# First attention: rotary queries from the 64-wide latent on two row tiles, and normalized rows ahead of their products

## The chip, the cores and the metric

The kernel runs on one core of a Trainium2 chip. The metric is the device time of one execution in microseconds, as the median of several runs.

## The reference

Four attention layers alternate with four feed-forward layers over 16 sequences of 256 tokens, 128 wide, each followed by a residual and a layer norm. The change is in the first attention:

```python
kv_c = x @ W_kv                                  # 32 wide
kv_c = kv_c * rsqrt(mean(kv_c * kv_c) + EPS) * g_kv
q_c = x @ W_q                                    # 64 wide, the query latent
k_content, v = heads(kv_c @ W_kdec, 8), heads(kv_c @ W_vdec, 8)
q_content = heads(q_c @ W_qdec, 8)
k_rope, q_rope = rope(heads(x @ W_krope, 32)), rope(heads(q_c @ W_qrope, 32))
q, k = concat(q_content, q_rope), concat(k_content, k_rope)
attn = softmax(where(causal, q @ k / sqrt(40), -inf))
x = layernorm(x + (attn @ v) @ W_o)
```

`rope(t) = t * cos + rotate_half(t) * sin`: the kernel multiplies by the weights and by the same weights with their halves swapped, multiplies each result by its table, and adds.

## The kernel before

X holds the tokens as 32 tiles of 128 rows and XT the same turned; the eight PSUM banks are four for scores (`sbank`), two for turned probabilities (`tbank`), one for values (`O`) and one for projections (`PRE`).

`opening_stage` loads the constants, the weights `l0_kv` and `l0_fold` and X in four parts. PE folds products of weights (W_q with the content part and with both rotary matrices, 128 x 640 and 128 x 512, in banks 5 to 7) and DVE copies them out. PE then transposes X in eight groups of four tiles, ACT copies them to XT, and the small latents give the root mean squares `rkv`. The last three groups reuse the banks of the fold and wait for its copies.

`narrow_stage` runs the attention. A sequence has three quads of four units: quads 0 and 1 take the late query tile (two heads of 256 keys per unit), quad 2 the early one (four heads of 128 keys). The loops run over 16 sequences, two in an iteration of the hardware loop, with one slot per quad. Every engine has its own instruction stream, in an order written out by hand in its `slot` function; semaphores join them, and all counts are offset by the constant CREDIT (1).

In a slot, PE issues the scores of its quad (`scores`, L747), the values of the quad two slots back, and the turns of the probabilities of the quad one slot back (`turn`, two before and two at the end of the slot). Between these stand the twelve steps that prepare the next sequence, four in each quad at places 0 to 3. `LatentNarrow` lists them: rms (root mean squares, spread over the rows), cq (content queries), ck (content keys), q and k (rotary queries and keys in four chunks each, two matmuls of 256 columns per step), v (values). Even steps use bank `PRE` (lane 0, `step_out0`), odd ones bank `sbank[0]` (lane 1, `step_out1`), so the scores of a slot wait until the lane-1 step before them has been read. ACT copies rms and cq out, DVE the others: for q and k one multiplication by the table of a whole bank into `tt` (two buffers), which POOL adds into `q` or `kx`.

DVE's slot: masks of units 0 and 1, step place 0, mask 2, place 1, mask 3, place 2, then what a finished tile of rows needs, and place 3. A tile `e` goes through four things in consecutive slots: its values are gathered and its denominators turned (`denominators`, DVE `recip`); POOL repeats the reciprocals, PE turns them (`repeat_turn`), and DVE multiplies the rows by them (`norm`, L923, into the one buffer `on`); PE projects them (`project`, L812), and DVE adds the residual (`residual`). Tiles end in quads 1 and 2. The two waits that matter here are in `norm` and `project`:

```python
dve.wait_ge(S["projected"], 4 * i + e + CREDIT)       # norm(e): tile e-1 is projected
pe.wait_ge(S["normed"], 4 * i + e + 1 + CREDIT)       # project(e)
```

`norm(e)` and `repeat_turn(e)` stand in quads 1 and 2, `project(e)` and `residual(e)` one slot later, in quads 2 and 0. So quad 2 holds the norm of one tile and the projection of the tile before. PE's order there is place 3, `repeat_turn`, `project`, turns 2 and 3; DVE's is place 2, place 3, `norm`, `residual`. The scores of the next slot wait for the residual and the norm that precede them, since banks 2 and 3 are used for them. POOL subtracts the row maxima of four units (`shift`) with the steps' adds between, and at the end of quad 2 copies the inputs of the sequence after next.

Of the kernel before, what the change touches and what calls it, by code (L numbers as in the profile page):

```python
# [139 lines left out]
def place_weights(items, region_cols):  # L140
# [257 lines left out]
def opening_stage(core, ctx, F, rkv, next_weights=()):  # L398
# [9 lines left out]
    with ExitStack() as mem:  # L408
# [10 lines left out]
        for name, rows, cols in (("wqT", 64, 128), ("wqall", 64, 640), ("wqrot", 64, 512), ("wkvT", 32, 128), ("wkdec", 32, 128),  # L419
                                 ("wvdec", 32, 128), ("gkv", 32, 1)):  # L420
            fold[name] = all_fold[0:rows, at:at + cols]
            at += cols
# [70 lines left out]
        def _(dve):  # L493
# [124 lines left out]
def narrow_stage(core, ctx, n, hd, steps, epilogue, next_weights=(), head_bias=False, weights_of=None):  # L618
# [13 lines left out]
    with mem:  # L632
# [111 lines left out]
        def _(pe):  # L744
# [92 lines left out]
            def step(i, b, j, first=False):  # L837

                seq = 2 * i + b
                if not first:  # L840
                    pe.wait_ge(S[steps.out_of(j)], steps.nth_out(seq, j) - 1 + CREDIT)
                    if j % lanes:
                        masks_done(i, b * NQ - NQ + j * NQ // NS, 0)
                elif j >= len(FIRST):
                    pe.wait_ge(S[steps.out_of(j)], steps.nth_out(0, j - len(FIRST)) + CREDIT)
# [11 lines left out]
            def slot(i, s):  # L857
# [19 lines left out]
                for e in ending(i, s, LRT):  # L877
                    repeat_turn(i, s, e)
# [12 lines left out]
        def _(dve):  # L891
# [62 lines left out]
            def step(i, b, j, first=False):  # L954
                seq = 2 * i + b
                if steps.engine[j] == "dve":
# [4 lines left out]
                    if steps.roped and steps.kinds[j] in "qk":  # L961
                        dve.wait_ge(S["rope_added"], seq * steps.ropes + max(steps.rank(j) - 1, 0) + CREDIT)
# [19 lines left out]
            def slot(i, s):  # L982
# [5 lines left out]
                if in_loop(i):  # L988
# [3 lines left out]
                    if lanes == 2:  # L992
                        steps_in(i, s, 2)
# [7 lines left out]
                for e in ending(i, s, LRT):  # L1001
                    norm(i, e)
# [147 lines left out]
class NarrowSteps:  # L1150
# [3 lines left out]
    ropes = 0  # L1154
    content = False
# [26 lines left out]
    def nth_out(self, seq, j):  # L1182
        return seq * (self.count // self.lanes) + j // self.lanes + 1

# [118 lines left out]
class LatentNarrow(NarrowSteps):  # L1303
# [5 lines left out]
    lanes = 2  # L1309

    def __init__(self, hd, rkv, F):
        self.kinds = ["rms", "cq", "ck"] + ["q", "q", "k", "k"] * 2 + ["v"]
        self.engine = ["act", "act", "dve"] + ["dve"] * 9
        self.hd, self.rkv, self.F = hd, rkv, F

    def alloc(self, sb, sem, B, S):
# [5 lines left out]
        B["tt"] = [sb(f"tt{i}", [P, 2, SEQ]) for i in range(2)]  # L1322
        B["rms_diagonal"] = [sb(f"rms_diagonal{i}", [P, 2, P]) for i in range(2)]
        B["rms"] = [sb(f"rms{i}", [P, SEQ]) for i in range(2)]
# [11 lines left out]
    def wait_q_and_k(self, pe, S, seq, q):  # L1336
        if q == 0:
            pe.wait_ge(S["k_ready"], seq + 1 + CREDIT)
            pe.wait_ge(S["rope_added"], 8 * seq + 4 + CREDIT)
# [3 lines left out]

    def pe(self, pe, core, B, S, PRE, j, b, seq):
        kind, F, xs = self.kinds[j], self.F, B["xs"][b]
        if kind == "rms":
            pe.wait_ge(S["diagonal"], seq + 1 + CREDIT)
            return pe.matmul(PRE[:, 0:SEQ], core.const("ones"), B["rms_diagonal"][b][:, :, :], start=True, stop=True)
        if kind in ("cq", "ck"):
            w = F["q"][:, 0:P] if kind == "cq" else F["kc"][:, :]  # L1350
            return pe.matmul(PRE[:, 0:SEQ], w, xs[:, :], start=True, stop=True)
# [5 lines left out]
        w = F["q"][:, P + c:P + c + P] if kind == "q" else weight(core, 0, "l0_wkrope")[:, c:c + P]  # L1357
        rot = F["qrot"][:, c:c + P] if kind == "q" else weight(core, 0, "l0_wkrot")[:, c:c + P]
        pe.matmul(PRE[:, 0:SEQ], w, xs[:, :], start=True, stop=True)
        return pe.matmul(PRE[:, SEQ:2 * SEQ], rot, xs[:, :], start=True, stop=True)  # L1360

    def act(self, act, core, B, S, PRE, j, b, seq):
        if self.kinds[j] == "rms":
            return act.activation(B["rms"][b][:, :], PRE[:, 0:SEQ], ACT.Copy)
        return act.activation(B["qc"][b][:, :], PRE[:, 0:SEQ], ACT.Copy, scale=-1.0 / math.sqrt(40.0))

    def dve(self, dve, core, B, S, PRE, j, b, seq):
        kind = self.kinds[j]
        if kind == "ck":
            dve.wait_ge(S[self.out_of(0)], self.nth_out(seq, 0) + CREDIT)  # L1370
            dve.wait_ge(S["k_ready"], seq + CREDIT)
            return dve.tensor_tensor(B["ck"][:, 0, :], PRE[:, 0:SEQ], B["rms"][b][:, :], ALU.mult)
        if kind == "v":
            for t in range(2):
# [4 lines left out]
        return dve.tensor_tensor(B["tt"][self.rank(j) % 2][:, :, :].rearrange("p a b -> p (a b)"), PRE[:, :],  # L1379
                                 core.const("rope32" + kind), ALU.mult)  # L1380

    def pool(self, pool, core, B, S, j, b, seq):
# [4 lines left out]
        if kind in "qk":  # L1387
            pool.wait_ge(S[self.out_of(j)], self.nth_out(seq, j) + CREDIT)
            tt = B["tt"][self.rank(j) % 2]
            dst = B["q"][b] if kind == "q" else B["kx"][b]  # L1390
# [2236 lines left out]
```

## Time and profile before

| | us |
|---|---|
| median of 3 runs (2693.41 to 2694.88) | 2693.76 |
| the profiled execution | 2698.68 |
| its span, first to last instruction | 2696.9 |
| PE busy | 2321.5 (86%) |
| DVE busy | 1825.7 (68%) |
| ACT busy | 1442.7 (53%) |
| POOL busy | 1354.2 (50%) |

The first attention takes the stretch from the start to about 472 us. The shares are means over all stages; the rows further down are of this stretch. A row of the timeline gives start, duration, engine, line, operation, what is written from what, shapes, the number of instructions merged in it, and in brackets the engine's idle time before it with what ended it. A float32 matmul is two instructions. Matmuls overlap with their successors, so the cost of one is read from the start of what follows and not from its duration; the same holds for DVE, whose operations start before the last one has ended.

### The profile page before, as it was taken

The page shows a single profiled execution, that of the slowest core. Times are in us where ns is not written, and L with a number is a line of the kernel's source. Part 1 is how long each engine was busy: PE and PEld are TensorE (multiplying, and loading weights), DVE is VectorE, ACT ScalarE, POOL GpSimd, SP SyncE. Part 2 cuts the span into 40 slices and gives each one's busy share as a digit, 9 for nine tenths or more (in the row PEclk, how much of TensorE's full clock was granted, in tenths as well). Part 3 has the DMA queues.
Part 4 walks back from the last instruction along what each step waited for, and adds up shares of the span by engine and source line. Part 5 has one row for each costly group of instructions (what it writes and reads, how often), then busy time and mean ns, then how long its engine had stood idle before and what let it go on. Part 6 is the DMA issues. An engine that isn't in the chain of part 4 may idle for free. (4 is left out here: it accounts for less than half of the span.)

```text
span 2696.9 us, 72182 instructions
## 1 busy us (share of the span) xinstructions
PE 2321.5 (86%) x21404; PEld 1819.3 (67%) x21404; DVE 1825.7 (68%) x8013; ACT 1442.7 (53%) x3445; POOL 1354.2 (50%) x1540
## 2 busy tenths in 40 slices
PE   7999999795999925889998889678978999999986
PEld 5777777363676625767776677567766777777755
DVE  4777776563888843568887599846646677777746
ACT  2445444222777713567775466445546666666614
POOL 4778776001777724368885455423314455544501
PEclk8999999796999967899998999899989999999978
DMA  2000000322000014600001000000000000000001
GB/s 76 3 0 0 0 0 0 85 62 100 3 0 0 0 65 137 189 2 1 0 0 41 2 1 0 0 2 1 0 24 1 2 0 0 0 0 0 0 1 32
DMA packets 44039, 55.98 MB, mean 21 GB/s; under 512 B 6800, under 2 KB 29417, under 8 KB 43564
## 3 DMA queue, kind: packets, MB, share of 16 engines
q1 hardware_dynamic: 41580, 49.37, 6.3%
q0 software_dynamic: 2304, 4.79, 0.5%
q8 instruction: 67, 1.10, 0.2%
q14 instruction: 88, 0.72, 0.1%
HBM read 47.11 MB, written 9.74 MB: 21 GB/s over the span
## 5 line engine op out<-in xcount | busy, mean ns | idle before, releaser
L1110 POOL TENSOR_TENSOR a_sm<-a_sm,a_top 128x512 f32<-128x512 f32 x512 | 521.0, 1042 | 170.7 <-DVE a_top L908 170.6
L908 DVE CUSTOM_DVE_ANT_0 a_sm<-bank,cst 128x128 f32<-128x128 f32 (+1 forms) x1024 | 296.8, 353 | 101.8 <-PE bank L770 84.1
L1033 ACT ACTIVATE a_pr<-a_sm 128x512 f32<-128x512 f32 x512 | 310.3, 629 | 78.7 <-PE bank L784 47.9
L1043 ACT ACTIVATE a_pt<-bank 128x512 f32<-128x512 f32 x432 | 240.5, 591 | 143.4 <-PE bank L784 140.6
L2935 POOL TENSOR_TENSOR a_pr<-a_sm,a_rden 128x512 f32<-128x512 f32 x192 | 197.2, 1049 | 228.3 <-DVE a_rden L2721 227.8
L784 PE MATMUL bank<-cst,a_pr 128*128 128x128 f32 x2304 | 308.2, 277 | 0.6 <-ACT a_pt L1043 0.2
L784 PEld LDWEIGHTS bank<-cst,a_pr 128*128 128x128 f32 x2304 | 257.8, 142 | 31.7 <-issue 20.6
L804 PEld LDWEIGHTS bank<-a_pt,a_v 128*32 128x32 f32 x4608 | 119.1, 110 | 110.8 <-issue 89.3
L2695 DVE CUSTOM_DVE_ANT_0 a_sm<-bank,cst 128x256 f32<-128x256 f32 (+1 forms) x512 | 149.9, 353 | 52.4 <-PE bank L2579 45.2
L804 PE MATMUL bank<-a_pt,a_v 128*32 128x128 f32 x4608 | 156.5, 276 | 29.3 <-issue 22.0
L908 DVE CUSTOM_DVE_ANT_0 a_sm<-bank,a_bias 128x256 f32<-128x256 f32 (+1 forms) x512 | 146.2, 354 | 30.7 <-PE bank L770 28.5
L3011 PE MATMUL bank<-a_xs,W 128*128 128x256 f32 x544 | 141.9, 396 | 16.9 <-ACT a_q L3024 10.8
L2935 POOL TENSOR_TENSOR a5h_pr<-a5h_sm,a5h_rden 128x512 f32<-128x512 f32 x64 | 65.7, 1047 | 149.8 <-DVE a5h_rden L2721 149.8
L908 DVE DVE_READ_ACCUMULATOR2_ANT a_top<- 128x1 f32 x1536 | 128.0, 83 | 0.0
L2841 ACT ACTIVATE a_sm<-a_sm,a_top 128x256 f32<-128x256 f32 x256 | 127.1, 505 | 0.0
L1100 POOL COPY a_xs<-XT 128x256 f32 (+1 forms) x54 | 21.7, 403 | 209.1 <-SPq L632 209.1
L916 DVE COPY a_pt<-bank 128x512 f32<-128x512 f32 x144 | 99.6, 692 | 38.3 <-PE bank L784 34.1
L3011 PEld LDWEIGHTS bank<-a_xs,W 128*128 128x128 f32 x544 | 96.8, 194 | 41.1 <-ACT a_q L3024 17.6
L1048 ACT ACTIVATE a_osb<-bank 128x256 f32<-128x256 f32 (+1 forms) x96 | 43.8, 456 | 145.9 <-PE bank L804 145.9
L770 PE MATMUL bank<-a_kx,a_q 32*128 32x512 f32 (+1 forms) x896 | 111.5, 580 | 9.4 <-DVE a_top L908 4.7
L2855 ACT ACTIVATE a_on<-bank 128x512 f32<-128x512 f32 x64 | 38.3, 598 | 147.3 <-PE bank L2611 147.3
L2579 PE MATMUL bank<-a_k,a_q 64*128 64x256 f32 (+1 forms) x1024 | 98.6, 337 | 17.8 <-ACT a_k L3024 9.4
(492 smaller groups left out, 5937.8 us busy)
## 6 DMA issues: line engine op xcount, KB each, us to landing
f_w<-in_l_w SPq DMA_DIRECT2D x40, 256.0 KB, 3.3
f_spread<-gate_rows SPq DMA_DIRECT2D x16, 512.0 KB, 6.8
W<-in_l_w SPq DMA_DIRECT2D x2, 2048.0 KB, 9.7
x_sorted<-in_l_blank SPq DMA_DIRECT2D x4, 660.0 KB, 7.6
f_xin<-x_sorted SPq DMA_DIRECT2D x10, 264.0 KB
X<-in_x SPq DMA_DIRECT2D x4, 512.0 KB, 7.5
a_bias<-bias_rows SPq DMA_DIRECT2D x1, 2048.0 KB, 7.8
X<-y_rows SPq DMA_DIRECT2D x8, 256.0 KB, 4.9
```

What stands on the lines that cost most here:

```text
L770: mm = pe.matmul(sbank[j][:, col:col + m * kw], B["q"][b][r0:r0 + rows, c, qt * P:(qt + 1) * P], B["kx"][b][r0:r0 + rows, x:x + m, 0:kw], ...
L784: mm = pe.transpose(tbank[j % 2][:, c * P:(c + 1) * P], pr[j][:, c * P:(c + 1) * P], ident)
L804: mm = pe.matmul(O[32 * group:32 * group + 32, blk * P:(blk + 1) * P], B["v"][b][:, kb, hd.slot[h], :], pt[j][:, col:col + P], start=(kb = ...
L908: ins = dve.tensor_tensor_reduce(sm[j][:, m * kw:(m + 1) * kw], sbank[j][:, m * kw:(m + 1) * kw], mk, 1.0, 3.0e38, ALU.add, ALU.min, top[: ...
L916: dve.tensor_copy(pt[j][:, :], tbank[j % 2][:, :]).then_inc(S[f"turned_out{j}"], 1)
L1033: act.activation(pr[j][:, :], sm[j][:, :], ACT.Exp, scale=-1.0).then_inc(S["probs"], 1)
L1043: act.activation(pt[j][:, :], tbank[j % 2][:, :], ACT.Copy).then_inc(S[f"turned_out{j}"], 1)
L1110: pool.tensor_tensor(whole, whole, top[:, qt, a:a + m].unsqueeze(2).to_broadcast([P, m, kw]), ALU.subtract).then_inc(S["shifted"], 1)
L2695: ins = dve.tensor_tensor_reduce(sm[s % 2 * 4 + j][:, m * kw:(m + 1) * kw], sbank[j][:, m * kw:(m + 1) * kw], mk, 1.0, 3.0e38, ALU.add, AL ...
L2841: ins = act.activation(part, part, ACT.Exp, bias=top[:, s % 2, j, m:m + 1], scale=-1.0, accum_out=den[:, s % 2, j, m:m + 1])
L2935: pool.tensor_tensor(pr[j][:, :].rearrange("p (h k) -> p h k", k=kw), sm[q % 2 * 4 + j][:, :].rearrange("p (h k) -> p h k", k=kw), rden[:, ...
L3011: mm = pe.matmul(bank[:, c * SEQ:(c + 1) * SEQ], w[:, a:a + P], xs[:, :], start=True, stop=True)
```

## The change

The rotary queries are no longer computed from the tokens with folded 128-row weights, but in two steps from the latent q_c, 64 wide. `l0_wqq` holds W_q twice, so one matmul of 256 columns in the rms step gives the latent in rows 0 to 63 and again in rows 64 to 127; ACT copies rms and latent out together (`rms_latent`, 512 columns). `l0_wqr` holds the rotary weights in its upper 64 rows and those with swapped halves in its lower 64. `pair` does two chunks at once: four matmuls of 64 rows, alternately on the upper and the lower row tile, each tile into a bank of its own (lane 0 and lane 1). DVE's two products then take one bank each, a table half repeated over both chunks, and POOL adds both chunks in one operation of 512 columns. There are three `tt` buffers instead of two.

The order of the steps becomes rms, cq, q, q in quad 0, ck, k, q, q in quad 1 and k, k, k, v in quad 2. PE issues a pair at place 2 and nothing at place 3; DVE has its two products at places 2 and 3. For this attention `repeat_turn` moves ahead of place 2 on PE and `norm` ahead of place 2 on DVE. The fold of the rotary queries is gone from the opening (two matmuls, two copies), `l0_fold` shrinks from 416 to 160 KB, and only the last transposed group waits for the copies of the fold. Two other attentions use `narrow_stage` with one lane; their order stays.

```diff
 WEIGHTS = {
-    0: [("l0_kv", 128, 36), ("l0_fold", 64, 1665), ("l0_wkrope", 128, 512), ("l0_wkrot", 128, 512),
+    0: [("l0_kv", 128, 36), ("l0_fold", 64, 641), ("l0_wqq", 128, 128), ("l0_wqr", 128, 512), ("l0_wkrope", 128, 512), ("l0_wkrot", 128, 512),
...
@@ opening_stage, PE and DVE @@
-            pe.matmul(bank[5][:, :], fold["wqT"], fold["wqall"][:, P:], start=True, stop=True).then_inc(folded, 1)
-            pe.matmul(bank[6][:, :], fold["wqT"], fold["wqrot"], start=True, stop=True).then_inc(folded, 1)
-            pe.matmul(bank[7][:, 0:P], fold["wqT"], fold["wqall"][:, 0:P], start=True, stop=True)
+            pe.matmul(bank[7][:, 0:P], fold["wqT"], fold["wqdec"], start=True, stop=True)
...
-                if g >= 5:
-                    pe.wait_ge(folded_out, g - 4 + CREDIT)
+                if g == GROUPS - 1:
+                    pe.wait_ge(folded_out, 1 + CREDIT)
...
-            dve.tensor_copy(F["q"][:, P:], bank[5][:, :]).then_inc(folded_out, 1)
-            dve.wait_ge(folded, 2 + CREDIT)
-            dve.tensor_copy(F["qrot"][:, :], bank[6][:, :]).then_inc(folded_out, 1)
-            dve.wait_ge(folded, 3 + CREDIT)
-            dve.tensor_copy(F["q"][:, 0:P], bank[7][:, 0:P])
+            dve.tensor_copy(F["qc"][:, :], bank[7][:, 0:P])
...
@@ narrow_stage, PE: step @@
-                steps.pe(pe, core, B, S, FIRST[j % len(FIRST)] if first else LANE[j % lanes], j, b % 2, seq).then_inc(S["step_mm"], 1)
+                banks = [FIRST[k % len(FIRST)] if first else LANE[k % lanes] for k in together]
+                if len(together) == 2:
+                    steps.pair(pe, B, S, banks, j, b % 2, seq).then_inc(S["step_mm"], 2)
+                elif together:
+                    steps.pe(pe, core, B, S, banks[0], j, b % 2, seq).then_inc(S["step_mm"], 1)
...
@@ narrow_stage, PE: slot @@
+                if lanes == 2:
+                    for e in ending(i, s, LRT):
+                        repeat_turn(i, s, e)
                 if in_loop(i):
                     steps_in(i, s, 2)
...
@@ narrow_stage, DVE: step and slot @@
-                        dve.wait_ge(S["rope_added"], seq * steps.ropes + max(steps.rank(j) - 1, 0) + CREDIT)
+                        dve.wait_ge(S["rope_added"], seq * steps.ropes + max(steps.rank(j) - steps.products + 1, 0) + CREDIT)
...
                     mask(i, s, 3)
-                    if lanes == 2:
+                if lanes == 2:
+                    for e in ending(i, s, LRT):
+                        norm(i, e)
+                    if in_loop(i):
                         steps_in(i, s, 2)
...
@@ LatentNarrow @@
-        self.kinds = ["rms", "cq", "ck"] + ["q", "q", "k", "k"] * 2 + ["v"]
-        self.engine = ["act", "act", "dve"] + ["dve"] * 9
+        self.kinds = ["rms", "cq", "q", "q", "ck", "k", "q", "q", "k", "k", "k", "v"]
+        self.engine = ["act", "act"] + ["dve"] * 10
...
+    def pair(self, pe, B, S, banks, j, b, seq):
+        pe.wait_ge(S[self.out_of(0)], self.nth_out(seq, 0) + CREDIT)
+        for k in range(2):
+            c = self.chunk(j + k) * P
+            for upper in range(2):
+                rows = slice(64 * upper, 64 * upper + 64)
+                mm = pe.matmul(banks[upper][:, k * SEQ:(k + 1) * SEQ], self.wqr[rows, c:c + P],
+                               B["rms_latent"][b][rows, 1, :], start=True, stop=True)
+        return mm
...
@@ LatentNarrow.act, dve and pool @@
-            return act.activation(B["rms"][b][:, :], PRE[:, 0:SEQ], ACT.Copy)
+            return act.activation(B["rms_latent"][b][:, :, :].rearrange("p a t -> p (a t)"), PRE[:, :], ACT.Copy)
...
+        half = self.chunk(j) % 2
+        return dve.tensor_tensor(tt[:, :, :], PRE[:, :].rearrange("p (a b) -> p a b", a=2),
+                                 over(core.const("rope32q")[:, half * SEQ:(half + 1) * SEQ], [P, 2, SEQ], 1), ALU.mult)
...
+        if kind == "q" and self.chunk(j) % 2:
+            c = self.chunk(j)
...
+            pool.tensor_tensor(B["q"][b][:, c - 1:c + 1, :], B["tt"][0][:, :, :], B["tt"][1][:, :, :], ALU.add
+                               ).then_inc(S["rope_added"], 2)
```

## Rows read from the trace of the kernel before

**Rows 1.** The page, its first line.
```profile
span 2696.9 us, 72182 instructions
```

**Rows 2.** Busy time by stretch, first attention: PE, PEld, DVE, ACT, POOL, clock, DMA share, GB/s.
```profile
220.00:260.00 40.00, 39.68 (x431) 31.61 (x424) 30.61 (x139) 20.64 (x42) 33.00 (x39) 1.00 0.00 0
```

**Rows 3.** Waits, 60 to 380 us: waiter, releaser, us in total, times, longest.
```profile
PEld bank L763 <- DVE a_tt L1379: 4.5, 11, 0.4
```

**Rows 4.** Timeline of PE: start, duration, line, operation, matmul instructions, idle before.
```profile
120.60 1.14 PE L763 MATMUL bank<-a_kc,a_qc 32*128 32x512 f32 x8
...
124.71 1.04 PE L784 MATMUL bank<-cst,a_pr 128*128 128x128 f32 x8
125.59 0.60 PE L1351 MATMUL bank<-a_xs,folded_kc 128*128 128x256 f32 x2
...
126.24 0.60 PE L1359 MATMUL bank<-a_xs,folded_q 128*128 128x256 f32 x2
...
127.11 0.61 PE L817 MATMUL bank<-W,a_on 128*128 128x128 f32 x4
...
128.51 1.14 PE L763 MATMUL bank<-a_kc,a_qc 32*128 32x512 f32 x8
...
134.36 0.60 PE L1359 MATMUL bank<-a_xs,W 128*128 128x256 f32 x2
...
137.76 1.14 PE L763 MATMUL bank<-a_kc,a_qc 32*128 32x512 f32 x8 [0.20 <-DVE a_on L926]
...
145.17 0.61 PE L817 MATMUL bank<-W,a_on 128*128 128x128 f32 x4
145.62 1.04 PE L784 MATMUL bank<-cst,a_pr 128*128 128x128 f32 x8
146.77 1.14 PE L763 MATMUL bank<-a_kc,a_qc 32*128 32x512 f32 x8
```

**Rows 5.** Timeline of DVE, the same sequence.
```profile
127.40 0.69 DVE L1379 TENSOR_TENSOR a_tt<-bank,W 128x512 f32<-128x512 f32 x1 [0.40 <-PE bank L1360]
...
128.01 0.28 DVE L344 TENSOR_TENSOR X<-bank,X 128x128 f32 x1
...
137.21 0.41 DVE L926 TENSOR_TENSOR a_on<-a_osb,bank 128x256 f32<-128x256 f32 x1
...
144.79 0.69 DVE L1379 TENSOR_TENSOR a_tt<-bank,W 128x512 f32<-128x512 f32 x1
...
145.40 0.60 DVE L1375 TENSOR_SCALAR a_v<-bank,rkv 128x128 f32<-128x128 f32 x2
...
145.92 0.41 DVE L926 TENSOR_TENSOR a_on<-a_osb,bank 128x256 f32<-128x256 f32 x1
146.25 0.28 DVE L344 TENSOR_TENSOR X<-bank,X 128x128 f32 x1
```

**Rows 6.** Timeline of PE in a later stage, eight matmuls of 64 rows.
```profile
1802.53 2.00 PE L2579 MATMUL bank<-a5h_k,a5h_q 64*128 64x256 f32 x16
1804.46 1.97 PE L2611 MATMUL bank<-a5h_pt,a5h_v 128*64 128x128 f32 x32
```

**Rows 7.** Opening: busy time by stretch, landing of X, timeline of PE and DVE.
```profile
8.00:13.00 5.00, 5.00 (x10) 2.60 (x10) 1.68 (x4) 0.00 (x0) 0.00 (x0) 1.00 1.20 290
18.10:22.20 4.10, 2.67 (x28) 2.19 (x24) 0.00 (x0) 2.17 (x4) 0.00 (x0) 1.00 0.47 177
...
DMA to landing us min/median/max: 6.3/7.5/8.7
...
18.11 1.09 PE L470 MATMUL bank<-cst,X 128*128 128x128 f32 x8
...
26.82 0.35 DVE L513 RECIPROCAL rkv<-open_std 128x32 f32<-128x32 f32 x1 [0.30 <-ACT open_std L490]
```

**Rows 8.** Groups of POOL between 30 and 580 us: busy us, mean ns.
```profile
L1110 POOL TENSOR_TENSOR a_sm<-a_sm,a_top 128x512 f32<-128x512 f32 x192 | 196.6, 1042 | 84.7 <-DVE a_top L908 84.7
...
L1391 POOL TENSOR_TENSOR a_k<-a_tt 128x256 f32<-128x256 f32 x68 | 49.9, 734 | 0.5
```

More of the change, by code:

```diff
@@ L418, in opening_stage @@
         all_fold, at, fold = weight(core, 0, "l0_fold"), 0, {}
-        for name, rows, cols in (("wqT", 64, 128), ("wqall", 64, 640), ("wqrot", 64, 512), ("wkvT", 32, 128), ("wkdec", 32, 128),
-                                 ("wvdec", 32, 128), ("gkv", 32, 1)):
+        for name, rows, cols in (("wqT", 64, 128), ("wqdec", 64, 128), ("wkvT", 32, 128), ("wkdec", 32, 128), ("wvdec", 32, 128),
+                                 ("gkv", 32, 1)):
             fold[name] = all_fold[0:rows, at:at + cols]
@@ L839, in step @@
                 seq = 2 * i + b
[L840 to L845, printed above, removed]
+                together = steps.together(j)
+                for k in together:
+                    if not first:
+                        pe.wait_ge(S[steps.out_of(k)], steps.nth_out(seq, k) - 1 + CREDIT)
+                        if k % lanes:
+                            masks_done(i, b * NQ - NQ + k * NQ // NS, 0)
+                    elif k >= len(FIRST):
+                        pe.wait_ge(S[steps.out_of(k)], steps.nth_out(0, k - len(FIRST)) + CREDIT)
                 if j == 0:
                     pe.wait_ge(S["x_copied"], seq + 1 + CREDIT)
-                steps.pe(pe, core, B, S, FIRST[j % len(FIRST)] if first else LANE[j % lanes], j, b % 2, seq).then_inc(S["step_mm"], 1)
+                banks = [FIRST[k % len(FIRST)] if first else LANE[k % lanes] for k in together]
[3 more added lines that the diff above has]
+                    steps.pe(pe, core, B, S, banks[0], j, b % 2, seq).then_inc(S["step_mm"], 1)
             for j in range(NS):
@@ L876, in slot @@
                     steps_in(i, s, 3)
-                for e in ending(i, s, LRT):
-                    repeat_turn(i, s, e)
+                if lanes == 1:
+                    for e in ending(i, s, LRT):
+                        repeat_turn(i, s, e)
                 if lanes == 2:
@@ L991, in slot @@
                     mask(i, s, 3)
-                    if lanes == 2:
+                if lanes == 2:
+                    for e in ending(i, s, LRT):
+                        norm(i, e)
+                    if in_loop(i):
                         steps_in(i, s, 2)
@@ L1000, in slot @@
                     steps_in(i, s, 3)
-                for e in ending(i, s, LRT):
-                    norm(i, e)
+                if lanes == 1:
+                    for e in ending(i, s, LRT):
+                        norm(i, e)
                 if lanes == 2:
@@ L1154 @@
     ropes = 0
+    products = 2
     content = False
@@ L1183, in nth_out, with together @@
         return seq * (self.count // self.lanes) + j // self.lanes + 1
+    def together(self, j):
+        return [j]
     def rank(self, j):
@@ L1321, in alloc @@
         B["ck"] = sb("ck", [P, 1, SEQ])
-        B["tt"] = [sb(f"tt{i}", [P, 2, SEQ]) for i in range(2)]
+        B["tt"] = [sb(f"tt{i}", [P, 2, SEQ]) for i in range(self.products)]
         B["rms_diagonal"] = [sb(f"rms_diagonal{i}", [P, 2, P]) for i in range(2)]
-        B["rms"] = [sb(f"rms{i}", [P, SEQ]) for i in range(2)]
+        B["rms_latent"] = [sb(f"rms_latent{i}", [P, 2, SEQ]) for i in range(2)]
         S["diagonal"] = sem("diagonal")
@@ L1346, in pe @@
         if kind == "rms":
+            pe.matmul(PRE[:, SEQ:2 * SEQ], weight(core, 0, "l0_wqq"), xs[:, :], start=True, stop=True)
             pe.wait_ge(S["diagonal"], seq + 1 + CREDIT)
@@ L1349, in pe @@
         if kind in ("cq", "ck"):
-            w = F["q"][:, 0:P] if kind == "cq" else F["kc"][:, :]
-            return pe.matmul(PRE[:, 0:SEQ], w, xs[:, :], start=True, stop=True)
+            return pe.matmul(PRE[:, 0:SEQ], F["qc" if kind == "cq" else "kc"][:, :], xs[:, :], start=True, stop=True)
         if kind == "v":
@@ L1371, in dve @@
             dve.wait_ge(S["k_ready"], seq + CREDIT)
-            return dve.tensor_tensor(B["ck"][:, 0, :], PRE[:, 0:SEQ], B["rms"][b][:, :], ALU.mult)
+            return dve.tensor_tensor(B["ck"][:, 0, :], PRE[:, 0:SEQ], B["rms_latent"][b][:, 0, :], ALU.mult)
         if kind == "v":
@@ L3520, in lay_out @@
     qr, kr = v["L0_attn_W_qrope"], v["L0_attn_W_krope"]
-    fold = [v["L0_attn_W_q"].T, content(v["L0_attn_W_qdec"]), qr, half_swapped(qr, 16, 32), v["L0_attn_W_kv"].T,
+    fold = [v["L0_attn_W_q"].T, content(v["L0_attn_W_qdec"]), v["L0_attn_W_kv"].T,
             content(v["L0_attn_W_kdec"]), in_value_order(L0_HEADS, v["L0_attn_W_vdec"]), v["L0_attn_g_kv"].reshape(32, 1)]
```

37 lines of the change are left out of this document (22 added, 15 removed).

## The prediction

> **What bounds the kernel now.** I read the page's first lines for the span [rows 1], then the busy time by stretch [rows 2]: between 220 and 260 us TensorE (PE) is busy 39.68 of 40 us at a granted clock of 1.00, VectorE (DVE) 30.61, GpSimd (POOL) 33.00, ScalarE (ACT) 20.64. The first attention is bound by PE, and DVE and POOL have about a fifth of their time free. The waits [rows 3] show the only PE gap that repeats: 11 times between 60 and 380 us, 4.5 us in all, the head of one quad in three waits for DVE's last product; there the normalization is named too, with 0.20 (the row of 137.76 in [rows 4]). Then I laid one sequence out by PE's starts [rows 4]: quad 0 from 120.60 to 128.51 (7.91 us), quad 1 to 137.76 (9.25), quad 2 to 146.77 (9.01), 26.17 in all, 16 times. Against the same starts stand DVE's last operations of each quad [rows 5].
>
> **Latencies read from these rows.** The last rotary matmul's successor starts at 127.11 [rows 4] and DVE's product of it at 127.40 [rows 5]: 0.29 from the end of streaming to DVE. The normalization ends at 137.21 + 0.41 = 137.62 and the scores start at 137.76: 0.14. After a residual the scores start later: 146.25 + 0.28 = 146.53 to 146.77, 0.24, and 128.01 + 0.28 = 128.29 to 128.51, 0.22. A 128x512 product lasts 0.69 but the next DVE operation starts 0.61 after it (127.40 to 128.01); a normalization takes 0.33 (145.92 to 146.25), the two value operations 0.52 (145.40 to 145.92).
>
> **PE's work.** A rotary step of full height is two 256-column matmuls and takes 127.11 - 126.24 = 0.87 us; four of them carry queries, 3.48 per sequence. The change does two steps as a pair of four matmuls, 64 rows high, on alternate halves of the array. The nearest rows are the eight matmuls of that height and width in a later stage [rows 6]: 1804.46 - 1802.53 = 1.93 us for eight, so 0.97 for four where full height takes 1.74. I take 0.87 of streaming, 0.14 to enter and 0.10 to leave; bounds 0.97 and, if the halves don't overlap, 1.98. The new latent matmul is 256 columns, half a step, 0.43. PE has per sequence 2 x (1.74 - 1.1) - 0.43 = 0.85 us less work.
> The Trainium skill (TensorE: Matmul & The Clock Gate, Part 3) gives a pack the time of one matmul and about 4 ns for each further tile; by that a pair would take 0.87 and the total would be some 3 us lower. The 1.93 us of [rows 6] is above it, and TensorEngine Tiling (Key Properties) says that a change of tiling mode drains the engine, which the pair does twice.
>
> **Quad by quad.** I follow what each quad's end waits for. The scores of the next quad wait for the last lane-1 product, since they write its bank, and for the residual where there is one.
> Quad 0 (latent and rms, content queries, the first pair). Turns 0 and 1 end at 125.59 [rows 4]; the new matmul moves this by 0.43 to 126.02, the pair streams until about 127.0. ScalarE's copy of rms grows from 256 to 512 columns, and its copy of the content queries behind it ends at about 125.9; that is hidden by the same two turns, and if that cover goes it costs the 0.2 it grows. Now DVE: first product at 127.29, reciprocal, 0.17, second product at 128.07, residual at 128.68, end 128.96, scores at 129.19. So 8.59 us instead of 7.91: +0.68. PE alone would be ready at 127.1 + 0.22 + 0.44 + 0.88 + 0.14, about 128.8 (0.22 for the denominators, 126.24 - 126.02; 0.44 for a projection, 145.62 - 145.17; 0.88 for two turns, 125.59 - 124.71).
> Quad 1 (content keys, a key step, the second pair). Turns 0 and 1 end 134.36 - 128.51 = 5.85 into the quad; a query step there becomes the content key matmul (-0.43), the turned reciprocals come ahead (+0.22): 5.64. The pair also needs the key step's product out of bank 0, at about 5.7. It streams until 6.6, products at 6.9 and 7.7 with the reciprocal between, scores at 8.55. Before: 9.25, so -0.70. The normalization, ahead of these products now, falls in DVE's wait for the pair and costs nothing. POOL takes the spread of the content keys (1024 columns, some 1.9 us at a shift's rate) between two of its shifts here; its four shifts of 1.04, an add of 0.73, one of 1.04 for both queries [rows 8] and the spread are about 8.1 us of this quad's 8.55, and the neighbours have 5.5 and 7.4: late by 1.2, with over 2 us before the turns of the next quad want it. Nothing on the path.
> Quad 2 (three key steps, values). Here two tiles meet. The normalization of the late tile waits until the projection of the tile before it has read `on` (there is one buffer), and that projection is issued in this same quad, behind PE's last two steps, ending 145.62 - 137.76 = 7.86 into it [rows 4]. Now the normalization is the last but one thing DVE does (145.92), so the wait hides behind two steps. The change puts it before them. DVE is through its masks by 144.79 at the latest, 7.03 into the quad [rows 5], without the queue behind it having anything to wait for. It now stands until 7.86 + 0.29 = 8.15; queued behind are the third key product, the values and the residual, and behind these the next scores. Normalization to 8.48, product to 9.09, values to 9.61, residual ends 9.89, scores at 10.12: +1.11 over 9.01. It needs an earlier tile, so 15 times.
> Sum for the stage: quad 0, 14 x 0.68 and two without residual at 0.35, +10.2; quad 1, 16 x -0.70 = -11.2; quad 2, 15 x 1.11 = +16.7. Total +15.7. An error of 0.1 in the pair moves it by 3.2.
> The Trainium skill (TensorEngine Tiling, PSUM Bottleneck) warns that tiling speeds TensorE up and not the evacuation of PSUM, which can then become the limit. By it alone quads 0 and 1 would lose what I give them; the rows agree, since the products last 0.69 each and PE has 1.2 to 1.6 us to hide them in.
>
> **The opening.** Two of the fold matmuls and their copies go, and 256 KB of 416 leave the queue ahead of X. At the 290 GB/s of [rows 7] that is 0.9 us. X's parts are issued at 3.23, 3.85 and 4.47 and land 6.3 to 8.7 us later; the third, the slowest, at 13.2, moved up at 12.3. Then come four transposes (0.9) and the first latent matmuls (1.0), so the next transposes start at 14.3 where they start at 18.11 now: -3.8. Between 18.10 and 22.20 PE has 2.67 us of work at a granted 1.00; at half that clock it takes 2.6 longer, and the gain is 1.2. I take -3.3, bounds -1.2 and -4.2.
> **The first sequence's steps**, ahead of the first scores. The latent copy delays the first product, and three products are in flight; POOL's eight adds of 0.73 become four and two of 1.04. Chained by hand from these durations the scores start 0.25 later; bounds -0.4 and +0.8. The two loads added (64 and 256 KB, against 256 taken from another) end long before the stage starts: nothing. The tail: nothing, bound 0.3 either way.
>
> **Total.** +15.7 - 3.3 + 0.25 = +12.6. The profiled execution took 2698.68 us, its span 2696.9 and 1.8 around it; it would become 2711.3. It lies 4.9 above the median of the three runs, 2693.76, so the median becomes 2706.4.
>
> **Rivals.**
> 1. PE's work alone decides, what a count of PE's instructions promises: DVE's products and the normalization stay hidden. Then quad 0 ends at about 8.2 (+0.3), quad 1 at 7.95 (-1.30), quad 2 at 8.87 (-0.14): -1.14 x 16 = -18, with the opening -21, 2672.5. For it speaks PE's 39.68 of 40; against it that DVE reaches the normalization 0.8 us before the projection has ended. It decides for this side if the projection ends more than 1 us earlier in quad 2. Chance 0.06.
> 2. The normalization costs nothing but the pair's products stay exposed: +10.2 - 11.2 - 2 - 3 = -6, 2688. Chance 0.10.
> 3. The half-height matmuls don't overlap: each pair takes 0.9 to 1.0 more, in front of DVE's two products, in quads 0 and 1: +30, 2736. Against it stands the 1.93 us of [rows 6]. Chance 0.05.
> 4. The stall of quad 2 is half of mine (another operation already fills it) and the opening gives its full 4.2: +3, 2697. Chance 0.09.
> The forecast itself has 0.70. Its own range by the bounds of the terms is 2699 to 2714; with rival 4 and the upper pair cost it is 2695 to 2715. What can be told from no change here is 0.2%, 5.4 us. Faster (below 2688.4) has 0.11, same 0.13, slower (above 2699.1) 0.76.
>
> **What would show it.** In the profile after: the scores' wait at the head of quad 0 named after DVE's residual or values, about 1.1 us in 15 of 16; DVE idle before the normalization, released by the projection, about 1.3 us each; quad 1 about 0.7 us shorter; pairs of about 1.0 us; the first transposes before 9 us and the end of the opening by 24. If quad 2 isn't longer, the central step is wrong; if the pairs take 1.9, rival 3.

## The result

The changed kernel takes 2706.35 us (median of 6, 2701.04 to 2707.03) where the kernel before takes 2693.91 (median of 6, 2692.87 to 2697.4): ratio 1.0038, interval 1.0028 to 1.0048. It is slower by 12.4 us. The profiled execution took 2707.03 with a span of 2705.3, 8.35 more than that of before; the profiled execution of before lies 4.8 above its own median, that of after 0.7.

The page's first lines say it as [rows 1] did: PE has less to do (2309.1 us, 2321.5 before), and the span is longer.

```profile
span 2705.3 us, 72259 instructions
## 1 busy us (share of the span) xinstructions
PE 2309.1 (85%) x21434; PEld 1798.9 (66%) x21434; DVE 1818.1 (67%) x8011; ACT 1446.3 (53%) x3445; POOL 1352.0 (50%) x1506
```

The busy time by stretch, PE, PEld, DVE, ACT, POOL, then the clock (the stretch of [rows 2]): PE has gone from 39.68 to 37.20 busy us of 40 at the same clock of 1.00. So PE no longer bounds the first attention throughout.

```profile
220.00:260.00 40.00, 37.20 (x431) 28.70 (x430) 29.43 (x147) 17.79 (x36) 30.30 (x36) 1.00 0.00 0
```

The waits between 60 and 380 us (who waited, for whom, us in total, times, longest) name what stands in its place. [rows 3] had 4.5 us at the head of a quad. Now the scores (L757) wait for three things of DVE, and DVE's normalization (L930) for the projection (L811).

```profile
DVE a_tt L1416 <- PE bank L1391: 25.9, 24, 1.7
...
DVE a_on L930 <- PE bank L811: 13.0, 11, 1.3
...
PEld bank L757 <- DVE a_tt L1416: 10.5, 22, 0.6
...
PE bank L757 <- DVE X L344: 7.3, 6, 1.2
PEld bank L757 <- DVE a_v L1408: 6.4, 5, 1.3
...
PE bank L757 <- DVE a_v L1408: 5.8, 6, 1.1
```

PE's timeline of one sequence, to lay beside [rows 4]. Quad 0 runs from 119.58 to 128.07, quad 1 to 136.53, quad 2 to 146.63: 8.49, 8.46 and 10.10 us, where 7.91, 9.25 and 9.01 stood.

```profile
119.58 1.14 PE L757 MATMUL bank<-a_kc,a_qc 32*128 32x512 f32 x8 [1.08 <-DVE a_v L1408]
...
125.09 1.14 PE L1391 MATMUL bank<-a_rms_latent,W 64*128 64x256 f32 x8
126.16 0.44 PE L820 MATMUL bank<-cst,a_osb 128*128 128x128 f32 x2
...
128.07 1.14 PE L757 MATMUL bank<-a_kc,a_qc 32*128 32x512 f32 x8 [0.16 <-issue]
...
133.80 1.14 PE L1391 MATMUL bank<-a_rms_latent,W 64*128 64x256 f32 x8
134.87 0.44 PE L820 MATMUL bank<-cst,a_osb 128*128 128x128 f32 x2
...
136.53 1.14 PE L757 MATMUL bank<-a_kc,a_qc 32*128 32x512 f32 x8 [0.35 <-DVE a_tt L1416]
...
143.93 0.61 PE L811 MATMUL bank<-W,a_on 128*128 128x128 f32 x4
144.38 1.04 PE L778 MATMUL bank<-cst,a_pr 128*128 128x128 f32 x8
146.63 1.14 PE L757 MATMUL bank<-a_kc,a_qc 32*128 32x512 f32 x8 [1.22 <-DVE X L344]
```

And DVE's, beside [rows 5]. The pair's two products (L1416) and the residual of quad 0; the two products of quad 1; in quad 2 the normalization, the third key product, the values and the residual.

```profile
126.38 0.69 DVE L1416 TENSOR_TENSOR a_tt<-bank,W 128x512 f32<-128x512 f32 x1 [1.71 <-PE bank L1391]
...
127.15 0.63 DVE L1416 TENSOR_TENSOR a_tt<-bank,W 128x512 f32<-128x512 f32 x1
...
127.69 0.28 DVE L344 TENSOR_TENSOR X<-bank,X 128x128 f32 x1
...
135.07 0.69 DVE L1416 TENSOR_TENSOR a_tt<-bank,W 128x512 f32<-128x512 f32 x1 [0.55 <-PE bank L1391]
...
135.84 0.63 DVE L1416 TENSOR_TENSOR a_tt<-bank,W 128x512 f32<-128x512 f32 x1
...
144.65 0.42 DVE L930 TENSOR_TENSOR a_on<-a_osb,bank 128x256 f32<-128x256 f32 x1 [1.17 <-PE bank L811]
144.99 0.68 DVE L1414 TENSOR_TENSOR a_tt<-bank,W 128x512 f32<-128x512 f32 x1
...
145.59 0.60 DVE L1408 TENSOR_SCALAR a_v<-bank,rkv 128x128 f32<-128x128 f32 x2
...
146.11 0.28 DVE L344 TENSOR_TENSOR X<-bank,X 128x128 f32 x1
```

The normalization starts at 144.65, 0.27 after the projection has streamed (144.38), and has waited 1.17 us for it. Third key product, values and residual follow without a gap, the residual ends at 146.39 (146.11 + 0.28), and the scores start 0.24 later; PE had been idle for 1.22 us by then. In quads 0 and 1 the same is seen on a smaller scale: the products start 0.22 and 0.20 after the pair (126.16, 134.87), and the next scores come when the last of them, or the residual behind it, has ended.

The opening and the first scores (L757), against [rows 7]: the transposes (L468) start at 9.04, groups 5 and 6 at 14.64 for 18.11, the opening ends with the reciprocal at 22.08 for 26.82, and the first scores start at 40.02. They started at 43.77 before.

```profile
7.17 0.79 PE L443 MATMUL bank<-W 64*128 64x128 f32 x2 [7.17 <-DMA W<-in_l_fold]
...
9.04 4.53 PE L468 MATMUL bank<-cst,X 128*128 128x128 f32 x20
...
14.64 1.09 PE L468 MATMUL bank<-cst,X 128*128 128x128 f32 x8
...
22.08 0.35 DVE L507 RECIPROCAL rkv<-open_std 128x32 f32<-128x32 f32 x1 [0.29 <-ACT open_std L488]
...
40.02 1.14 PE L757 MATMUL bank<-a_kc,a_qc 32*128 32x512 f32 x8 [3.11 <-POOL a_k L1427]
```

### The profile page after: what moved, and what is told of

Read it like the earlier page. It is cut to its first block and busy times, and to the rows that moved or that the text cites. A ratio compares the mean times of both kernels' runs of the same rounds, so it can differ in the third digit from the quotient of the medians.

```text
span 2705.3 us, 72259 instructions
## 1 busy us (share of the span) xinstructions
PE 2309.1 (85%) x21434; PEld 1798.9 (66%) x21434; DVE 1818.1 (67%) x8011; ACT 1446.3 (53%) x3445; POOL 1352.0 (50%) x1506
## 5 line engine op out<-in xcount | busy, mean ns | idle before, releaser
L778 PE MATMUL bank<-cst,a_pr 128*128 128x128 f32 x2304 | 309.0, 277 | 0.6 <-ACT a_pt L1051 0.4
L778 PEld LDWEIGHTS bank<-cst,a_pr 128*128 128x128 f32 x2304 | 258.3, 142 | 31.7 <-issue 20.6
```

The lines of the kernel that those rows point to most:

```text
L778: mm = pe.transpose(tbank[j % 2][:, c * P:(c + 1) * P], pr[j][:, c * P:(c + 1) * P], ident)
```

## The experiments

Each kernel is compared with the kernel before on the same chip (medians 2694.56 for the first four, 2695.77 for the others). Behind each ratio stands its 95% interval. Differences from the changed kernel are between medians of separate sessions, between which the median of the kernel before itself moved by 0.7 (first four) and 1.9 us (the others). "Quad 0, 1, 2" are the steady distances between the starts of content scores, read off PE's timeline; the sums are over all 16 sequences.

### Two buffers for the normalized rows

```diff
-        on = sb("on", [P, cols])
+        ons = [sb(f"on{k}", [P, cols]) for k in range(lanes)]
...
-                dve.wait_ge(S["projected"], 4 * i + e + CREDIT)
-                dve.tensor_tensor(on[:, :], ...
+                dve.wait_ge(S["projected"], total(i, 4, e + 1 - lanes) + CREDIT)
+                dve.tensor_tensor(ons[e % lanes][:, :], ...
```

> The changed kernel with two buffers for the normalized rows in this attention (even and odd tiles), so that norm(e) waits for the projection of tile e-2 and no longer for e-1, which is issued in the same quad. Theory of the stall (the wait for the projection costs 1.1 us in quad 2, 15 times): quad 2 goes from 10.1 us back to about 9.0, the total from 2706.4 to about 2690 (0.9985 of before), and DVE's idle time before norm named after the projection falls from about 16 us to nearly 0. Rival (the norm costs by its place in DVE's queue alone, 0.33 us ahead of two steps): quad 2 stays above 9.7 and the total at 2701 or more.

Measured: 2688.32 us, ratio 0.9976 (0.9967 to 0.9986), 18.0 less than the changed kernel. Quad 2 went from 10.10 and 9.96, in turn, to 8.89 and 8.81; quads 0 and 1 kept 8.49 and 8.46. DVE's wait for the projection is gone from the list of waits. The timeline, the head of quad 2, its normalization, its projection and the next scores:

```profile
134.30 1.14 PE L757 MATMUL bank<-a_kc,a_qc 32*128 32x512 f32 x8 [0.35 <-DVE a_tt L1416]
...
141.18 0.42 DVE L930 TENSOR_TENSOR a_on<-a_osb,bank 128x256 f32<-128x256 f32 x1
...
141.71 0.61 PE L811 MATMUL bank<-W,a_on 128*128 128x128 f32 x4
...
143.20 1.14 PE L757 MATMUL bank<-a_kc,a_qc 32*128 32x512 f32 x8
```

The normalization (141.18) now starts ahead of the projection (141.71) and not behind it. The one wait that the change had uncovered is worth 18 us in the medians, more than the whole loss of 12.4. The traces say the same: the last residual of the stage is added at 463.40 us and no longer at 480.88. 1.4 of these 17.5 us are already there at the first scores, ahead of every normalization, so what the wait costs by the traces is about 16.

### Norm and turn back at their old places

```diff
 # PE slot
-                if lanes == 2:
-                    for e in ending(i, s, LRT):
-                        repeat_turn(i, s, e)
                 if in_loop(i):
                     steps_in(i, s, 2)
...
                 if in_loop(i) and lanes == 2:
                     steps_in(i, s, 3)
-                if lanes == 1:
-                    for e in ending(i, s, LRT):
-                        repeat_turn(i, s, e)
+                for e in ending(i, s, LRT):
+                    repeat_turn(i, s, e)
...
 # DVE slot
-                if lanes == 2:
-                    for e in ending(i, s, LRT):
-                        norm(i, e)
-                    if in_loop(i):
-                        steps_in(i, s, 2)
+                if in_loop(i) and lanes == 2:
+                    steps_in(i, s, 2)
...
                 if in_loop(i) and lanes == 2:
                     steps_in(i, s, 3)
-                if lanes == 1:
-                    for e in ending(i, s, LRT):
-                        norm(i, e)
+                for e in ending(i, s, LRT):
+                    norm(i, e)
```

> The changed kernel with norm and repeat_turn at their old places (behind place 3), all else as changed. Theory of the stall: quad 2 returns to about 9.0 us (-16.5 in all), quad 1 grows by the 0.33 us of the norm, which now stands between the pair's last product and the next scores (+5): 2695. Rival (the exposed products of the pair are what costs, the move nothing): 2706 as before.

Measured: 2692.93 us, ratio 0.9995 (0.9986 to 1.0005): no difference from before, and 13.4 below the changed kernel. Quad 2 returned to 9.01 to 9.07 and 8.87; quad 1 grew by 0.21 to 8.66, less than the 0.33 expected. So the new steps without the move, opening included, give a gain too small to be told here (1.6 us in the medians; 4.3 at the end of the stage in the traces): what they save in quad 1, 9.4 us in all, they give back in quad 0, 8.9.

### The move alone

```diff
 # PE slot, of the kernel before
+                if lanes == 2:
+                    for e in ending(i, s, LRT):
+                        repeat_turn(i, s, e)
                 if in_loop(i):
                     steps_in(i, s, 2)
...
-                for e in ending(i, s, LRT):
-                    repeat_turn(i, s, e)
+                if lanes == 1:
+                    for e in ending(i, s, LRT):
+                        repeat_turn(i, s, e)
...
 # DVE slot
-                    if lanes == 2:
+                if lanes == 2:
+                    for e in ending(i, s, LRT):
+                        norm(i, e)
+                    if in_loop(i):
                         steps_in(i, s, 2)
...
-                for e in ending(i, s, LRT):
-                    norm(i, e)
+                if lanes == 1:
+                    for e in ending(i, s, LRT):
+                        norm(i, e)
```

> The kernel before with norm and repeat_turn moved ahead of place 2 and nothing else. Theory of the stall: quad 2 grows from 9.0 to 10.1 us (+16.6 in all), quad 1 shrinks by 0.1 to 0.2 (-2): 2708. Rival (in the old order of steps DVE has enough to do, and the move only frees quad 1): 2690 to 2692.

Measured: 2706.24 us, ratio 1.0040 (1.0026 to 1.0054), 11.7 more than the kernel before. Quad 2 is 10.1 and 9.96 as in the changed kernel, quad 1 went from 9.25 to 9.05, quad 0 kept 7.91. The waits of this kernel between 60 and 380 us:

```profile
DVE a_on L930 <- PE bank L817: 13.0, 11, 1.3
...
PE bank L763 <- DVE X L344: 6.2, 5, 1.3
...
PE bank L763 <- DVE a_v L1383: 5.4, 5, 1.1
```

DVE's 13.0 us in 11 times and the scores' waits for residual and values are those of the changed kernel. The stall comes with the move and needs nothing of the new steps.

### Lane 1 first

On top of two buffers, DVE's slot takes the step of the other lane for queries:

```diff
                 for j in steps_at(s, place):
-                    step(i, s // NQ + 1, j)
+                    step(i, s // NQ + 1, j ^ 1 if lanes == 2 and steps.kinds[j] == "q" else j)
```

> The kernel with two buffers for normalized rows, and DVE takes the pair's product out of lane 1 first (the bank that the next scores write), lane 0 second. Theory (the scores wait for the second product alone): quad 1 goes from 8.46 to the time of PE's work, about 7.95 us, 16 times -0.5 = -8; quad 0 keeps its 8.5, since the residual still stands behind both products; 2682. Rival (PE's time per quad is not what would bound quad 1 then; POOL or the turned probabilities are next): quad 1 stays at 8.3 or more, 2688.

Measured: 2683.81 us, ratio 0.9958 (0.9941 to 0.9974), 4.5 less than with two buffers alone. Quad 1 went from 8.46 to 8.10 or 8.13, between the two expectations; quad 0 kept 8.49. Between 60 and 380 us the scores (L757) now wait for no operation of DVE, so quad 1 is as long as PE's work in it, which is 8.10 and not the 7.95 of the expectation.

### The residual between the products

On top of the kernel with two buffers and lane 1 first:

```diff
+                early = lanes == 2 and in_loop(i) and s % NQ == 0
+                if early:
+                    for e in ending(i, s, LY):
+                        residual(i, e)
                 if in_loop(i) and lanes == 2:
                     steps_in(i, s, 3)
...
-                if lanes == 2:
+                if lanes == 2 and not early:
                     for e in ending(i, s, LY):
                         residual(i, e)
```

> As the kernel with two buffers for normalized rows and lane 1 first, and in quad 0 DVE adds the residual between the pair's two products instead of behind both. Theory (quad 0's end is set by the residual): quad 0 goes from 8.49 us to the end of PE's turns, about 8.3, -3 in all, total 2681. Rival (nothing left there): no change, 2684. Against the kernel before about 0.995.

Measured: 2677.76 us, ratio 0.9932 (0.9916 to 0.9949), the fastest of all kernels here, 18.0 us faster than the kernel before on the same chip and 28.6 than the changed kernel. Quad 0 is 8.26. The timeline of the last turns (L778) and the residual of quad 0, then the starts of quads 1, 2 and 0:

```profile
146.27 1.04 PE L778 MATMUL bank<-cst,a_pr 128*128 128x128 f32 x8
...
146.60 0.29 DVE L344 TENSOR_TENSOR X<-bank,X 128x128 f32 x1
...
147.24 1.14 PE L757 MATMUL bank<-a_kc,a_qc 32*128 32x512 f32 x8
...
154.31 1.04 PE L778 MATMUL bank<-cst,a_pr 128*128 128x128 f32 x8
...
155.34 1.14 PE L757 MATMUL bank<-a_kc,a_qc 32*128 32x512 f32 x8
...
164.16 1.14 PE L757 MATMUL bank<-a_kc,a_qc 32*128 32x512 f32 x8
```

The residual (146.60 + 0.29) is done before the last turns have streamed (146.27 + 0.87), and the scores follow these by 0.10. In quad 1 they follow the last turns in the same way (154.31, 155.34). PE bounds all three quads again: between 220 and 260 us it is busy 39.95 of 40. Of the 6.0 us against the kernel of the last section (3 expected) the quads 0 hold 3.5. Most of the rest is one stretch: in that kernel's trace PE is idle for 2.59 us at about 90 us, for nothing that the profile shows, and the clock is 0.76 from 88 to 92; the kernel with two buffers alone has 2.40 us of it at about 91, this one has none. What causes it is open.

### Two product buffers

```diff
-    products = 3
+    products = 2
```

> The changed kernel with two buffers of rotary products instead of three. Theory (the third buffer is needed, because POOL's add of the key step in quad 1 comes behind the spread of the content keys): the pair's second product in quad 1 waits for that add, which ends at about 136.75 in the trace where the product starts at 135.84; quad 1 goes from 8.45 to about 9.4 us, +14 in all, 2720. Rival (POOL is ahead anyway, the third buffer is idle): 2706, no change.

Measured: 2726.62 us, ratio 1.0114 (1.0097 to 1.0131), 20 more than the changed kernel. Quad 1 is 9.45, 1.0 longer, and its 16 add up to 16.6 more; the first quad 0 and the first quad 2 are 1.0 and 1.6 longer, and the first scores start 19.5 us after the opening's reciprocal instead of 17.9. Part of these three is the clock, granted 0.70 between 58 and 62 us where the changed kernel has 1.00. The wait between 60 and 380 us is the expected one, of the pair's product for POOL's add of keys:

```profile
DVE a_tt L1416 <- POOL a_k L1427: 9.4, 11, 0.9
```

### All four matmuls on one half

```diff
-                mm = pe.matmul(banks[upper][:, k * SEQ:(k + 1) * SEQ], self.wqr[rows, c:c + P],
-                               B["rms_latent"][b][rows, 1, :], start=True, stop=True)
+                mm = pe.matmul(banks[upper][:, k * SEQ:(k + 1) * SEQ], self.wqr[0:64, c:c + P],
+                               B["rms_latent"][b][0:64, 1, :], start=True, stop=True)
```

> The changed kernel with all four matmuls of a pair on the lower 64 rows (the rotated half of the queries is computed from the unrotated weights, so that part of the computation is changed). Theory (the two row tiles run at the same time): a pair goes from 1.07 us to about 1.9, in front of DVE's products, so quads 0 and 1 grow by 0.8 to 0.9 each, +27 in all, 2733. Rival (the pair is bound by loading its weights or by changing the tiling, not by streaming): under +8.

Measured: 2738.14 us, ratio 1.0156 (1.0135 to 1.0176). A pair and its successor:

```profile
164.92 1.99 PE L1391 MATMUL bank<-a_rms_latent,W 64*128 64x256 f32 x8
166.84 0.44 PE L820 MATMUL bank<-cst,a_osb 128*128 128x128 f32 x2
```

166.84 - 164.92 = 1.92 us where the changed kernel has 126.16 - 125.09 = 1.07. Quads 0 and 1 are 9.34 and 9.30, 0.84 longer each. The two row tiles do overlap, and the 0.85 us that this saves lies fully on the path. The kernel is 31.8 us slower than the changed one; 26.9 of these are in quads 0 and 1.

### The fold matmuls and the old size of l0_fold

```diff
-    0: [("l0_kv", 128, 36), ("l0_fold", 64, 641), ("l0_wqq", 128, 128), ...
+    0: [("l0_kv", 128, 36), ("l0_fold", 64, 1665), ("l0_wqq", 128, 128), ...
...
+            for k in range(2):
+                pe.matmul(bank[5 + k][:, :], fold["wqT"], all_fold[0:64, 641 + 512 * k:641 + 512 * (k + 1)], start=True, stop=True)
...
```

> The changed kernel with l0_fold at its old 416 KB (the added columns are zeros) and two fold matmuls of 512 columns ahead of the others, into banks that are overwritten later. Theory (the opening's gain is PE's: 3.5 us of matmuls at the lower clock, and 0.7 from the earlier landing of the weights): the first transpose returns from 9.04 to about 13.1 us and the end of the opening from 22.1 to about 26.5; total +4.3. Rival of the prediction (X's landing is what the earlier transposes would meet): the opening ends within 3.8 of the changed kernel's.

Measured: 2709.36 us, ratio 1.0052 (1.0039 to 1.0065). The timeline of its opening:

```profile
8.03 3.78 PE L444 MATMUL bank<-W 64*128 64x512 f32 x4 [8.03 <-DMA W<-in_l_fold]
...
13.31 4.29 PE L470 MATMUL bank<-cst,X 128*128 128x128 f32 x20
...
26.10 0.35 DVE L509 RECIPROCAL rkv<-open_std 128x32 f32<-128x32 f32 x1 [0.29 <-ACT open_std L490]
```

The first transpose is back at 13.31 and the opening ends at 26.10, 4.0 later than in the changed kernel; 3.58 of these are the matmuls (8.03 to 11.61) and 0.86 the later landing of the weights (7.17 to 8.03). By the edge of 3.8 set for the rival this alone is a narrow verdict; clearer is that the changed kernel's transposes start at 9.04, right behind the fold, and not when X's landing would have let them. The median difference, 3.0, is smaller than the 4.0 of the traces, with executions of this kernel between 2703.6 and 2712.1.

## Why the prediction was right, point by point

The sum was 2706.4 and the median 2706.35, but the agreement to a tenth is luck. The stage was sized 2.5 us too high and opening and first steps together 0.7, both in the same direction: in the traces the three add up to +9.5 and not to +12.6. The medians are 12.4 apart because the profiled execution of before lies 4.8 above its own median. The forecast had put the profiled execution of the changed kernel at 2711.3, as far above its median; it took 2707.03, 0.7 above.

**What bounds the kernel.** Before the change PE did, as [rows 2] said. The step that carried the prediction was not PE's count but the order of waits at each quad's end.

**Quad 2.** Predicted +1.11 over 9.01; measured 10.10 and 9.96, in sum +15.5 (predicted 16.7). The prediction took the quad of 9.01 us; the quads alternate between 9.01 and 8.86 before, and both become 1.1 longer. The size for one is right; the count is not. The first quad 2 has no earlier tile and grows by 0.1 (8.61 to 8.67), the next fourteen carry the +15.4, and the last has no further quad behind it: from its scores to the layer norm it is +0.2. Inside the quad the links are as written: the projection ends 7.85 us into it (predicted 7.86), the normalization starts at 8.12 (8.15), the residual ends at 9.86 (9.89). Norm behind the projection, the queue behind the norm and the scores behind that are each seen in the timeline; one kernel takes the stall away with a buffer (-18.0 us), one gives it to the kernel before (+11.7). DVE's wait is 1.17 to 1.18 us each (13.0 in 11), where about 1.3 was named as a sign.

**Quad 0.** Predicted 8.59, measured 8.49. The sum came out as predicted, +10.2, by luck: a steady quad loses 0.58 and not 0.68, 7.5 in thirteen of them, and the first two, for which 0.35 each was taken, lose 2.07 and 0.68. Of the 2.07 some 1.4 are the clock. In this trace PE is idle for 3.11 us ahead of the first scores, the clock is 0.50 between 42 and 44 us, and the first quad 0 takes 8.39. With norm and turn at their old places the first quad, which has neither, holds the same work, PE is idle for 2.94 ahead of it, the clock is 1.00, and the quad takes 6.97 (6.32 before the change). The chain of the steady quad is as written: first product 6.80 us into the quad (6.69 predicted), second 7.57 (7.47), residual 8.11 (8.08). Its last link is shorter: the scores start 0.10 after the residual has ended (127.69 + 0.28 = 127.97, then 128.07), where 0.22 to 0.24 was read from [rows 5]. In quad 2 that link is 0.24 again.

**Quad 1.** Predicted 8.55 and -11.2, measured 8.45 and -12.6. Products at 7.00 and 7.77 (6.9 and 7.7), and the scores 0.06 after the last of them where 0.14 was taken.

**The pair.** 1.07 us (125.09 to 126.16) and 0.10 ahead of it, 1.17, where 1.11 was predicted for both; [rows 6] gave 0.97 for four matmuls inside a run of eight. The row on a later stage was good enough; one half alone takes 1.92, 1.8 times as long. The Trainium skill (TensorEngine Tiling, Overview) gives up to twice as the speedup for a contraction of 64; the trace stays below it. One sum of the prediction is off: by the span model that it names, 0.87 for the pair and not 1.11, the total would be 7.7 lower by its own 3.2 for each 0.1, and not "some 3 us"; nothing else in the forecast used it.

**The stage in sum.** The layer norm behind the stage starts at 474.95 in the trace of before and at 484.43 in that of after; from the first scores to it are 431.2 and 444.4 us: +13.2, predicted +15.7. This term was sized too high by 2.5, 1.2 in quad 2 and 1.4 in quad 1. Without the 1.4 us that the low clock adds to the first quad 0, which was not forecast, it would be +11.8.

**The opening.** Predicted -3.3, measured -4.7 between the two traces and -4.0 against the 26.10 of the kernel with the fold matmuls put back. The step that failed is its mechanism: the landing of X's third part at 12.3 was to set the start of what follows. The twenty transposes start behind the fold at 9.04 and take 4.5 us, 3.7 before; in this trace PE has no idle time for X between them; what the opening gains is PE's 3.6 us and the earlier weights. Groups 5 and 6 start 3.5 us earlier (14.64 for 18.11; predicted 3.8). The other 1.3 us come from the remainder, which took 7.4 us, 8.7 before: it did not slow down after the change, as the branch at the lower clock (-1.2) had it, but was slow before. The clock of before is 0.58 between 22 and 26 us, and its last latents and sums of squares take longer there than the 1.06 and 1.05 of the changed kernel, which has 1.00 up to 22 us:

```profile
22.18 1.55 PE L455 MATMUL bank<-XT,W 128*32 128x512 f32 x8 [0.69 <-ACT XT L484]
...
24.42 1.87 PE L461 MATMUL bank<-W,open_squares 128*128 128x4 f32 x8 [0.70 <-ACT open_squares L488]
```

**The first sequence's steps.** Predicted +0.25 with a bound of +0.8; measured +1.0 (22.08 to 40.02 against 26.82 to 43.77). POOL's add of both queries was sized at 1.04, a shift's time; it takes 1.27. The group of POOL operations:

```profile
L1432 POOL TENSOR_TENSOR a_q<-a_tt 128x512 f32<-128x512 f32 x34 | 43.3, 1273 | 9.2 <-DVE a_tt L1416 9.2
```

Two of these are 0.46 longer than assumed, against the missing 0.75; that both lie fully on the path was not shown, and the rest is not settled. With the opening the two terms gave -3.75 for the -3.05 predicted.

**From the traces to the medians.** Stage, opening and first steps add up to +9.5 in the traces, the spans differ by 8.4, the medians by 12.4. The profiled execution of before has the slow opening told above (26.82; the kernel with the move alone, which shares its instructions, 25.86, and first scores at 42.29 instead of 43.77), which can be 1.0 to 1.5 of its 4.8 us over the median. What makes up the rest is open: no other execution of it has a trace.

**Rivals.** Rival 1, 2672.5 by PE's work alone, was wrong for this kernel, but what it described exists: with the norm freed, the lanes swapped and the residual moved, the time is 2677.8, 5.3 above its price. It put quads 0, 1 and 2 at 8.2, 7.95 and 8.87; they are 8.26, 8.10 and 8.86 on average. Rival 2 (norm free, products exposed) gave 2688, and the kernel with two buffers, which is that case, took 2688.3. Rival 3, no overlap, gave 2736, and the kernel on one half took 2738.1; here the closeness is partly luck, since the +30 was for quads 0 and 1, which hold 26.9, and the rest lies ahead of the first scores. Rival 4, half the stall, is ruled out by the quads 2 that grew by 1.1 each.

**The rule against the change**, PSUM Bottleneck in the Trainium skill's TensorEngine Tiling, holds here: with the pair quads 0 and 1 end with the products of DVE and the residual behind them. The experiments add how it is lifted without a faster product: by reading first the bank that the next matmuls want (-4.5 us), and by moving the residual between the two products (-3.5 in the quads 0).

## What to carry to other kernels

When an operation is moved ahead in one engine's queue, look for its own waits first, and for where the releasing instruction stands in the other engine's queue at the new time; an operation whose wait was hidden behind two others can stall everything that it is put in front of. When matmuls are made faster, follow the last operation that reads their bank up to the next matmul that writes it: here quads 0 and 1 together were 0.2 us shorter than before with the pairs alone, and 0.8 shorter once DVE's order was changed. A second buffer of 256 columns, for the rows that the moved operation writes, turned a loss of 12 us into a gain of 6.

## What the runs showed that was not expected

POOL's addition of two 128x512 operands into a third tile takes 1.27 us (34 in the stage), while its subtraction of 128x512 with a repeated operand takes 1.04 ([rows 8]). Two 128x256 additions take 1.46, so merging them saves 0.19 and not 0.42.

The granted clock came up at different times. In the changed kernel it is 0.51 between 26 and 31 us and 0.96 between 31 and 42. In the kernel with all four matmuls on one half PE is busy without a gap from 30 us to 42, and the clock stays at 0.50 (1.2 GHz, the lower of its two levels, where 1.00 is 2.4) all the while; its first scores start at 46.2 us, 6.2 later. The two fences are the busy time by stretch (PE, PEld, DVE, ACT, POOL, clock, DMA share, GB/s), of the changed kernel and of the one on one half:

```profile
26.00:31.00 5.00, 4.75 (x14) 3.03 (x14) 0.00 (x0) 0.98 (x2) 1.02 (x3) 0.51 0.00 0
31.00:42.00 11.00, 7.89 (x52) 6.22 (x54) 6.00 (x11) 0.00 (x0) 7.13 (x7) 0.96 0.01 1
```

```profile
30.00:36.00 6.00, 6.00 (x14) 3.87 (x14) 2.17 (x4) 0.00 (x0) 1.94 (x2) 0.50 0.01 3
36.00:42.00 6.00, 6.00 (x15) 4.34 (x14) 2.12 (x4) 0.00 (x0) 3.19 (x4) 0.50 0.00 0
```

So a part of that kernel's 31.8 us over the changed one is the clock, in the 6.2 ahead of the first scores; the 26.9 in quads 0 and 1 are not touched by it in the steady quads. The 6.2 are not the clock alone: two pairs lie in them, at 3.71 us each (28.77 to 32.48, 35.34 to 39.05), where one half takes 1.92 at a clock of 1.00 and the changed kernel's two take 1.96 and 1.06. Why the clock rose later was not tried.
